# Taking 29 unread products out of TensorE's queue in the last stages of a conditioned attention and expert layer

## What is computed

```python
c   = einsum('bsi,boi->bso', x, weight[adapter_ids])       # a weight picked for the batch
x   = x + attention(c, Wq, Wk, Wv, Wo, cos, sin)           # 32 query heads, 8 key heads of 16, causal, rotary
y   = x @ W.T + 0.5 * (x @ lora_A[labeler]) @ lora_B.T     # low rank part picked for the batch
base   = y @ W_base.T + b_base
logits = y @ W_router.T                                    # 8 experts, the best 2 weighted by a softmax
out = x + base + 2 * sum(gate_e * (y @ A_e.T) @ B_e.T)     # experts of rank 16
```

## Time and profile before

| | us |
|---|---|
| median of 3 runs | 237.53 |
| lowest and highest of the 3 | 237.14, 239.57 |
| the profiled execution, whole | 237.22 |
| its span, first to last instruction | 235.4 |
| busy in the span: PE | 221.1 |
| busy in the span: DVE | 172.3 |
| busy in the span: ACT | 117.2 |
| busy in the span: POOL | 96.2 |

### The profile page before, as it was taken

One profiled execution on the slowest core, in us unless ns is written; L12 is line 12 of the kernel. 1 busy time (PEld: TensorE's weight loads), 2 busy tenths in 40 slices (PEclk: granted clock), 3 DMA queues, 4 the chain that ended last, 5 costly groups with the idle time before them and its releaser, 6 DMA issues.

```text
span 235.4 us, 5807 instructions
## 1 busy us (share of the span) xinstructions
PE 221.1 (94%) x2010; PEld 173.7 (74%) x2010; DVE 172.3 (73%) x905; ACT 117.2 (50%) x287; POOL 96.2 (41%) x110
## 2 busy tenths in 40 slices
PE   6699997998999999999999999999999999899893
PEld 6588885786778876877687778777876776477693
DVE  0599838947864997589757975898489849948873
ACT  3697442686586257526752675266622650171210
POOL 7020570857369074707480748064922320002020
PEclk9999999999999999999999999999999999999999
DMA  4999508007002602260116011601101010003011
GB/s 131 319 387 361 202 1 277 6 0 226 3 3 56 225 3 58 55 213 4 57 52 218 4 56 47 223 3 57 45 3 47 13 45 3 0 4 102 0 47 45
DMA packets 20050, 21.18 MB, mean 90 GB/s; under 512 B 6453, under 2 KB 11573, under 8 KB 20021
## 3 DMA queue, kind: packets, MB, share of 16 engines
q1 hardware_dynamic: 20020, 20.81, 27.4%
HBM read 18.71 MB, written 2.10 MB: 88 GB/s over the span
## 4 chain that ended last, share of the span: by engine, by line
PE 77%; DVE 12%; ACT 4%; issue 2%; DMA 2%; SPq 1%; DVEq 0%; ACTq 0%
PE bank L1125 14%; PE bank L1126 12%; PE bank L1130 12%; PE bank L1152 5%; PE bank L1216 4%; PE bank L1178 4%; PE bank L1231 3%; PE bank L1136 3%; DVE thrown L794 3%; PE bank L1233 2%; PE bank L1232 2%; DMA stage_d<-base_t 2%; PE bank L1310 2%; ACT late L472 2%; DVE qkv_w_lo L724 2%
## 5 line engine op out<-in xcount | busy, mean ns | idle before, releaser
L373 POOL TENSOR_TENSOR cond_w_lo<-cond_raw,cond_w_hi 128x512 fp32r<-128x512 f32 x28 | 35.5, 1291 | 48.1 <-ACT cond_w_hi L472 48.1
L794 DVE CUSTOM_DVE_ANT_0 thrown<-bank,causal 128x64 f32<-128x64 f32 (+1 forms) x256 | 47.3, 253 | 0.6 <-issue 0.5
L393 POOL TENSOR_TENSOR rope_b<-rope_a,rope_b 128x128 f32<-128x128 f32 (+1 forms) x16 | 16.1, 1021 | 25.9 <-DVE rope_b L850 25.9
L472 ACT ACTIVATE max_rows<-bank,own_p 128x128 fp32r<-128x128 f32 x32 | 9.2, 369 | 33.3 <-PE bank L1162 33.3
L402 POOL TENSOR_TENSOR x_bias<-x,bias_row 128x512 f32<-128x512 f32 x8 | 10.3, 1290 | 28.7 <-DVE out_sb L974 27.3
L1125 PE MATMUL bank<-qkv_w_hi,c_t_hi 128*128 128x256 f32 (+1 forms) x64 | 21.4, 352 | 0.4 <-DVE c_t_lo L724 0.3
L1125 PE MATMUL bank<-fused_w_hi,late 128*128 128x324 f32 (+2 forms) x68 | 20.6, 318 | 0.9 <-ACT late L472 0.2
L794 DVE DVE_READ_ACCUMULATOR2_ANT neg_max<- 128x1 f32 x256 | 21.3, 83 | 0.0
L1126 PE MATMUL bank<-qkv_w_lo,c_t_hi 128*128 128x256 f32 (+1 forms) x64 | 20.3, 338 | 0.0
L1126 PE MATMUL bank<-fused_w_lo,late 128*128 128x324 f32 (+2 forms) x68 | 19.7, 306 | 0.0
L472 ACT ACTIVATE cond_w_hi<-cond_raw 128x512 fp32r<-128x512 f32 x32 | 17.5, 622 | 1.0 <-DMA cond_raw<-cond_w_t 1.0
(11 more groups left out here) (166 smaller groups left out, 631.4 us busy)
## 6 DMA issues: line engine op xcount, KB each, us to landing
cond_raw<-cond_w_t SPq DMA_DIRECT2D x7, 1024.0 KB, 5.5
xt_raw<-x_t SPq DMA_DIRECT2D x8, 256.0 KB, 5.9
x_nat<-x SPq DMA_DIRECT2D x8, 256.0 KB, 2.6
out<-out_sb SPq DMA_DIRECT2D x8, 256.0 KB, 2.0
stage_d<-base_t SPq DMA_DIRECT2D x4, 256.0 KB, 4.8
cond_raw<-cond_w_t SPq DMA_DIRECT2D x4, 256.0 KB, 4.6
stage_b<-w SPq DMA_DIRECT2D x4, 256.0 KB, 5.5
stage_a<-w_q SPq DMA_DIRECT2D x4, 256.0 KB, 5.9
```

What stands on the lines that cost most here:

```text
L373: pool.tensor_tensor(cond_w.lo[:, k, :], cond_raw[:, k, :], f32(cond_w.hi[:, k, :]), ALU.subtract).then_inc(cond_lo, 1)
L393: pool.tensor_tensor(qk[:, at:at + w], rope_a[:, at:at + w], rope_b[:, at:at + w], ALU.add).then_inc(qk_ready, 1)
L472: return nc.scalar.activation(out, in_, ACT.Copy, scale=scale)
L794: nc.vector.tensor_tensor_reduce(thrown[:, b % 2, j, e, 0:width // 2] .rearrange("p (a s) -> p a s", a=h + 1), scores[:, :, e, :], causal[ ...
```

## The change

The four calls of `keep_busy` and the function are taken out. Nothing else is changed; no wait is added or removed, and every other instruction keeps its place in its queue.

```diff
-            def keep_busy(n):
-
-                for _ in range(n):
-                    nc.tensor.matmul(d_ps[:, 0:D - P], ident_b[:, :],
-                                     ident_b[:, :].unsqueeze(1).broadcast_to([P, PAIRS - 1, P]), start=True, stop=True)
-
...
             score(7, 2)
-            keep_busy(6)
             ffn_high(LAST - 2, 1, right_ps(LAST - 2))
             context(LAST - 1)
             ffn_low_half(LAST - 2, 1, right_ps(LAST - 2))
             score(LAST, 3)
-            keep_busy(12)
             transpose_maxima(LAST)
             passes_t(LAST, 0)
             mask_t(LAST, 0)
...
             context(LAST)
             transpose_x1(LAST - 1)
-            keep_busy(5)
             ffn_high(LAST - 1, 0, left_ps(LAST - 1))
             project_low(LAST - 1)
...
             transpose_x1(LAST)
             finish_ffn(LAST - 1)
-            keep_busy(6)
             project_low(LAST)
```

## The result

Without the 29 fillers the kernel takes 239.07 us, the median of 22 executions, against 237.50 us of the kernel before, also 22. The ratio is 1.0058, with a 95% interval of 1.0036 to 1.0080: slower by 1.4 us. (The medians stand 1.6 us apart; the ratios in this text compare only fast executions, which leaves out one of the 22, of 241.75 us.) The profiled execution took 238.27 us, 1.05 more than the one before; its span is 236.4 us against 235.4.

The account below looks back on a forecast made before the run. The prediction took TensorE to bound the kernel, with 77% of the chain that ended last. It summed 237.22 + 1.35 - 0.23 = 238.3, 238.6 by the median, and said 238.5 us, range 236.9 to 240.7.

Parts of the forecast that it names:

- Group one: 6 fillers at 196.37: later work moves forward, but the scores wait for DVE's maxima; worth 0.
- Group two: 12 fillers at 201.41: turning batch 7's maxima waits for line 806 anyway; worth 0, idle 3.31 us, not 0.97.
- Group three: 5 fillers at 213.59: `ffn_high(6, 0)` could start 0.09 us earlier, but DVE holds this stretch; worth 0.
- Group four: 6 fillers at 224.21: `project_low(7)` starts at 225.02, not 225.25, and this reaches the end; 0.23 us gained.
- The clock falls: In the idle time before batch 7's maxima are turned, TensorE's clock drops to half at about 203.7.
- 2.5 us behind the last product: Idle time before the clock's fall, read at the kernel's end and applied after the scores ending at 201.20.
- What a fall costs: On TensorE's path from 204.51: 0.9 us delay plus 0.45 until the clock rises at 208.4, sum 1.35 us.
- The delay at line 1336: Start of `ffn_rank(5, 1)`, 206.57 before, expected at 207.5 with the clock at half: 0.9 us later.
- The 0.8 us: Half-clock addition ahead of `less_maxima`, in the sum 0.15 + 0.8 - 0.16 = 0.8.
- rival (b): Clock stays down or falls again through `project_out(6)` and the exponentials' second half: 240.3, 240.6 by the median; chance 0.2.
- Rival (a): The clock holds, since the scores break the idle time: 237.0 to 237.3 us; chance 0.2.
- Rival (c): Fillers at all four places hold back real work through an occupied bank or full queue: 231.3, half 234.3; chance 0.02.

Follow-up runs that it names:

- e1: Kernel before with only the 12 fillers ahead of the turning of batch 7's maxima taken out, the other 17 kept: ratio 1.0068 to the kernel before.
- e4: Kernel before with the 12 fillers ahead of batch 7's maxima replaced by 40 unread products of 8 columns: ratio 1.0084 to the kernel before.
- e12: The changed kernel without the 29 fillers, unedited, profiled once more: this execution took 239.15 us, with a mean clock of 0.978.
- e8: Kernel before with 6 fillers in place of 12 ahead of batch 7's maxima, all else kept: ratio 1.0009 to the kernel before.
- e2: Kernel before with the calls of 6, 5 and 6 fillers out and only the 12 kept: ratio 1.0020 to the kernel before.
- e9: Kernel before without fillers, low products and rank product of batch 5's right half moved behind the block 3 scores: ratio 1.0103 to the kernel before.
- e6: Kernel before with all 29 fillers out and ten float32 fillers added at the start: ratio 1.0111 to the kernel before.
- e10: Kernel before with the work order of e9, 9 and 13 fillers in the idle times, the later calls of 5 and 6 kept: ratio 1.0006.
- e5: Kernel before with all 29 fillers kept and ten float32 fillers added in the waits at the start: ratio 1.0008 to the kernel before.

## Why the prediction came out as it did

The forecast was 238.5 us, slower by 0.4%; it is slower by 0.6%. Its steps, by the text on record:

- Group one, worth 0: right. The context moved forward, `score(7, 3)` waits 0.59 us for DVE (0.64 forecast), and line 806 is at 204.09.
- Group two, worth 0 by its time, 3.31 us of idle time: right, 3.25, and e1 shows that the clock is lost when this group alone is out.
- Group three, worth 0: right. ACT's copy ends at 214.78 + 0.60 = 215.38 and `ffn_high(6, 0)` starts at 215.53, 0.15 us behind it, as before (214.39 and 214.54).
- Group four, 0.23 us gained: wrong, the term is 0.03 at most. These rows of after, TensorE first, then DVE, show it:

```profile
226.20 0.71 PE L1310 MATMUL bank<-late 128*128 128x256 f32 x4 [0.86 <-DVE late L724]
```

```profile
225.25 0.69 DVE L724 TENSOR_TENSOR late<-bank,late 128x512 fp32r<-128x512 f32 x1 [1.05 <-ACT late L472]
```

  225.25 + 0.69 = 225.94, and the product starts 0.26 us later. Before it was 225.25 - 224.96 = 0.29. That is 0.03 us, no more than the spread between kernels that keep these fillers (3.12 to 3.16 us from line 1346 to line 1310). So that wait had ended last already then, and the fillers that filled the row up to it weren't on the path. I took the handover of 0.06 us from line 806, an operation of 32 columns, where this one has 512; the row of the right size stood in the trace before, behind line 893 (DVE, then TensorE):

```profile
222.09 0.69 DVE L893 TENSOR_TENSOR x<-bank,x_nat 128x512 f32<-128x512 f32 x1
```

```profile
223.01 0.60 PE L1136 MATMUL bank<-ident,x 128*128 128x128 f32 x4
```

  222.09 + 0.69 = 222.78, and 0.23 us to the next transposition. That the handover grows with the size is read from these two sizes only.
- The clock falls: right, as the slices of the changed kernel, e1, e4 and e12 show. That it falls 2.5 us behind the last product was wrong as a rule. It fell at 202.9 in e12, 1.6 us before the work resumed, and at 205.25 in the profiled execution after, 0.9 us behind the resumption; e8 and e2 lost it with 1.94 and 1.19 us idle. At the end of the kernel itself, where the rule came from, the fall came 2.3 us behind the last product in e9, 2.8 in the changed kernel, and in e2, e4 and e8 not in the 3.2 us up to the end of the span. So idle times shorter than the 2.5 us of the forecast can have a fall behind them too, and there the measurement decides.
- What a fall costs, 1.35 us: measured 1.16 in the profiled execution, 1.55 in e1 and 1.58 in e2 for a stretch of 3.4 us, and 1.88 in e12, 2.00 in e6 and 2.31 in e4 for one of 6.8. The delay at line 1336 was forecast as 0.9 us and is 0.29 (206.69 - 204.34 = 2.35, against 206.57 - 204.51 = 2.06 before), since the fall came later than taken; the products of `project_out(6)` paid the rest, at 0.43 us each in place of 0.23. The 0.8 us that the forecast adds for `passes_t` and `mask_t` was my estimate, and no run shows it: in e12, with the clock low from before line 1162, they hold 206.64 - 204.89 = 1.75 us, 0.55 more than the 1.2 before. `less_maxima` holds 207.35 - 206.64 = 0.71 us there against 0.44, 0.27 more and not 0.1, and the delay at line 1336 is 0.80 (207.35 - 204.49 = 2.86 against 2.06), near the 0.9. In the profiled execution the sum comes out at 238.3 as forecast against 238.27. That this agrees so closely is luck: a cost taken too high met a gain taken too high.
- The median is 0.6 us above the forecast. The prediction took one low stretch of about four microseconds for every execution, and gave rival (b), a longer one, a chance as one course for all; the runs show a mixture. 13 of 22 executions have more low time than one stretch of 3.4 us. In a part of them this is rival (b), as e12 shows, low up to 209.7; how large that part is isn't known without their profiles. Not all of the low time comes from the change: the kernel before has some in 24 of 83 executions by itself.
- Rival (a), the clock holds: in none of 55 executions without the full fillers. Rival (c), the fillers in front of real work: nothing of it, no kernel without fillers is faster.

What stays open: why the low stretch ends after about 3.4 us in one execution and 6.8 in another, and which low stretches the executions without a profile had, since they report only a mean. It changes from one execution to the next of the same kernel, and I found no row that tells in advance.

## What to carry to other kernels

Unread products in the idle time of TensorE can be worth more than they cost, where their end lies ahead of a wait that ends last anyway and the work behind is a chain on TensorE: here 12 of them, in 3.25 us of idle time, held the clock in most executions (59 of 83 of the kernel before kept a mean of 0.996 or more, and none of 55 without full fillers there); a low stretch in this place cost 1.0 (e9 against e10) to 2.3 us (e4) in the profiles. The 17 others were worth nothing that could be measured, though e2's interval leaves room for up to 0.45%. Before filler work is called a cost, look at when the operation that is waited for ends, and take the handover from a row of an operation of the same size. When the clock is in play, look at the distribution of the times and at the mean clock of each execution, not at one profile.

## What the runs showed of the hardware

- At the same idle time the clock may fall or hold: with 6 fillers and 1.94 us idle it fell in the profiled execution and held in 4 of 12, and with 12 fillers and 1.19 us it fell in e2's profile and held in 6 of 12 executions.
- Low stretches ahead of the last product came in two lengths in the profiles, 3.4 us (twelve of them) and 6.8 us (e4, e6, e12), and their price hangs on the place: one at 12 us delayed line 1162 by 0.8 us at most, one at 42 us by 1.2 (e9 against e10).
- It came down during work too: at 207.1 us in e2, 2.2 us after the work had resumed, and at 42 us in e5 behind two waits of 0.7 us.
- 40 products of 8 columns, each with its load of 128 columns of weights, took 1.16 us and kept the clock in none of 8 executions; 6 products of 384 columns in the same time kept it in 4 of 12.
